# Crossbar transposes for the later tiles of a second matrix layer, and a weight load that is moved behind a scatter

## What is computed

```
h = relu(layernorm(x))
x = x + gat(relu(gat(h, W1, att1, b1)), W2, att2, b2)
h = relu(layernorm(x))
x = x + gcn(relu(gcn(h, W3, b3)), W4, b4)

gat: h = h @ W;  e = leaky_relu((h @ att_src)[src] + (h @ att_dst)[dst]);  softmax of e over the edges of one dst
     out[dst] = sum of alpha * h[src];  + b
gcn: h = h @ W;  out[dst] = sum of h[src] / sqrt(deg[src] * deg[dst]);  + b
```

## Time and profile before

| what | value |
|---|---|
| median of 3 runs | 2192.77 us (2192.68 to 2198.5) |
| profiled execution, own time | 2194.5 us |
| its span, first to last instruction | 2192.7 us |
| TensorE busy | 2143.6 us, 98% of the span |
| VectorE, ScalarE, GpSimd busy | 1461.2, 947.1, 863.9 us |
| SyncE's DMA queue, GpSimd's DMA queue | 263.74 MB and 172.60 MB, 41.5% and 25.4% of the engines' span |

### The profile page before, as it was taken

The page is one execution under the profiler, slowest core; times in us unless marked ns, Lnnn a source line. Parts: engine busy times, 40 slices in busy tenths (PEclk is TensorE's granted clock), DMA queues, the critical chain, the costliest instruction groups (busy, mean ns, idle before and its releaser), DMA issues.

```text
span 2192.7 us, 35927 instructions
## 1 busy us (share of the span) xinstructions
PE 2143.6 (98%) x13355; PEld 1359.5 (62%) x13355; DVE 1461.2 (67%) x3322; ACT 947.1 (43%) x1289; POOL 863.9 (39%) x1067
## 2 busy tenths in 40 slices
PE   8999998899999999999999999999999999999997
PEld 4666665556666666666666666666666666666664
DVE  8998753435766764343889999665666667876563
ACT  4444454344545454333554444433334333333432
POOL 3212177524333321243654454443353413245462
PEclk9999999999999999999999999999999999999999
DMA  5988999995556554434755566666766747776562
GB/s 185 234 223 200 227 214 201 184 241 158 177 191 202 187 172 134 166 122 141 241 183 200 187 203 202 225 244 220 280 238 228 238 165 252 234 246 192 176 202 85
DMA packets 243091, 438.63 MB, mean 200 GB/s; under 512 B 138867, under 2 KB 139065, under 8 KB 242790
## 3 DMA queue, kind: packets, MB, share of 16 engines
q1 hardware_dynamic: 202550, 263.74, 41.5%
q0 software_dynamic: 40368, 172.60, 25.4%
HBM read 234.94 MB, written 179.89 MB: 189 GB/s over the span
## 4 chain that ended last, share of the span: by engine, by line
PE 90%; DVE 6%; issue 2%; ACT 1%; POOL 1%; POOLq 0%; DVEq 0%; ACTq 0%
PE ps_h L993 78%; PE ps_z L969 7%; PE ps_e L1069 1%; PE ps_e L1070 1%; DVE edge_mem L1246 1%; PE ps_e L1059 1%; PE ps_e L1060 1%; DVE bn L1156 1%; DVE z_lo L1208 1%; DVE res L1235 0%; DVE res L1225 0%; ACT z L876 0%; DVE pre L1174 0%; DVE pre L1172 0%; PE ps_e L1015 0%
## 5 line engine op out<-in xcount | busy, mean ns | idle before, releaser
L993 PE MATMUL ps_h<-w_hi,z_hi 128*128 128x384 f16 x2916 | 712.9, 326 | 1.6 <-DVE w_lo L1146 1.6
L993 PE MATMUL ps_h<-w_hi,z_lo 128*128 128x384 f16 x2916 | 712.9, 326 | 0.0
L993 PE MATMUL ps_h<-w_lo,z_hi 128*128 128x384 f16 x2916 | 712.9, 326 | 0.0
L863 ACT ACTIVATE row_out<-ps_h,grow 128x768 f32<-128x768 f32 x237 | 212.9, 898 | 647.5 <-PE ps_h L993 637.9
L1208 DVE TENSOR_TENSOR z_lo<-ps_z,z_hi 128x768 f16<-128x768 f32 x243 | 231.8, 954 | 353.2 <-ACT z_hi L868 352.8
L993 PEld LDWEIGHTS ps_h<-w_lo,z_hi 128*128 128x128 f16 x2916 | 285.5, 98 | 189.1 <-issue 0.7
L993 PEld LDWEIGHTS ps_h<-w_hi,z_lo 128*128 128x128 f16 x2916 | 285.5, 98 | 189.0 <-issue 0.7
L993 PEld LDWEIGHTS ps_h<-w_hi,z_hi 128*128 128x128 f16 x2916 | 285.2, 98 | 176.0 <-issue 20.8
L993 PE MATMUL ps_h<-w_hi,x_keep 128*128 128x384 f16 x1752 | 362.6, 327 | 14.0 <-issue 14.0
L993 PEld LDWEIGHTS ps_h<-w_hi,x_keep 128*128 128x128 f16 x1752 | 169.9, 98 | 127.9 <-issue 19.5
L685 POOL DMA_INDIRECT out<-res,perm_out x79 | 103.5, 1310 | 322.6 <-DVE res L1235 301.3
(11 more groups left out here) (223 smaller groups left out, 2515.6 us busy)
## 6 DMA issues: line engine op xcount, KB each, us to landing
rows<-row_out SPq DMA_DIRECT2D x199, 384.0 KB
rows<-e_out SPq DMA_DIRECT2D x60, 384.0 KB, 4.5
row_in<-in_x SPq DMA_DIRECT2D x40, 384.0 KB, 3.8
row_in<-rows SPq DMA_DIRECT2D x40, 384.0 KB, 4.3
x_rows<-pre SPq DMA_DIRECT2D x40, 384.0 KB, 3.8
res<-x_rows SPq DMA_DIRECT2D x40, 384.0 KB, 4.2
pure_rows<-row_out SPq DMA_DIRECT2D x39, 384.0 KB
row_in<-pure_rows SPq DMA_DIRECT2D x39, 384.0 KB, 5.1
```

The costliest lines, as they stand in the source:

```text
L863: nc.scalar.activation(pair(row_out[t.slot]), psum_pair(ps_h[t.slot]), ACT.Copy, scale=scale).then_inc(row_ready, 1)
L993: last = nc.tensor.matmul(ps_h[s][:, a, 0:HALF], zp[:, c, :], wp[:, c, a * HALF:(a + 1) * HALF], start=(c == 0 and zp is zh and wp is hi), ...
```

## The change

Tiles of layer 2 from g = 124 on are crossed as well. Their preparation on VectorE and their gather on GpSimd move one window ahead. The third weight's loads move from windows 53 to 58 to windows 65, 67, ... 75, its maxima from one in each window from 59 to every second window from 68, its joining matmul from window 70 to 79, its scale to 80. Bias 1 is loaded in window 66, biases 2, 3 and 4 in windows 89, 91 and 93, each with its own semaphore that its first user waits for; the attention vectors of layer 1 move from window 69 to 74. The wait for the parameters before the degrees is taken out. The maxima of the second weight start three windows later. The small diagonal matrix of `max_w` lies in `e_out`, and the small per-tile factors have eight slots in place of four. The diff, without the repeated changes of `slot4` to `slot8`:

```diff
-        self.slot, self.slot4 = g % 2, g % 4
+        self.slot, self.slot8 = g % 2, g % 8
-        self.crossed = layer == 1 and g >= FIRST_CROSSED
+        self.crossed = layer == 1 and g >= FIRST_CROSSED or layer == 2 and g >= SECOND_CROSSED
+SECOND_CROSSED = 124
+    W3_AT = SCATTERED + 1
-    max_at = {2: TURNED + 4, 3: ORDERED + 1, 4: begin["2m"] + 14}
+    max_at = {2: TURNED + 4, 3: W3_AT + 2 + 2 * KC, 4: begin["2m"] + 14}
-        w_diag = edge_mem[:, 15 * P:16 * P]
+        w_diag = e_out[:, 512:512 + P]
...
# SyncE
                 t = tile(w, 6)
-                if t and t.crossed:
+                if t and t.crossed and t.layer == 1:
                     load_x(t)
-            def load_params():
-                for n in (1, 2, 3, 4):
-                    sp.dma_start(bias_bc[n][:, :], row_of(bias[n])).then_inc(params_loaded, 16)
+            def load_bias(n):
+                sp.dma_start(bias_bc[n][:, :], row_of(bias[n])).then_inc(bias_loaded[n], 16)
-                if w == ORDERED:
-                    load_params()
+                for n, at in ((1, ORDERED - 3), (2, ORDERED + 20), (3, ORDERED + 22), (4, ORDERED + 24)):
+                    if w == at:
+                        load_bias(n)
+                if w == ORDERED + 5:
                     load_atts(1)
-                if MASKS + 6 <= w < MASKS + 6 + KC:
-                    load_w(3, w - MASKS - 6)
+                if W3_AT <= w < W3_AT + 2 * KC and (w - W3_AT) % 2 == 0:
+                    load_w(3, (w - W3_AT) // 2)
...
# GpSimd
                 t = tile(w, 4)
-                if t:
+                if t and not t.crossed:
+                    load(t)
+                t = tile(w, 5)
+                if t and t.crossed:
                     load(t)
...
# ScalarE, make_half
+                if t.layer == 1:
+                    (as before, with the layer norm's factors)
+                else:
+                    nc.scalar.activation(z_half[t.xn % 3][:, 0:D], input_of(t)[:, :], ACT.Relu,
+                                         scale=shrink[t.slot8][:, 0:1]).then_inc(half_ready, 1)
...
# VectorE
+                    if layer == 4:
+                        dve.wait_ge(e_stored, (ET + 1) * 16)
+            def pre_free(t):
+                ago = T[t.g - 2]
+                x_read(dve, ago)
-                wait(dve, z_ready, t.g - 1)
+                pre_free(t)
                 if not t.chain:
                     wait(dve, x1_stored[t.slot], t.x1_before * 16)
+                elif t.c < KEEP:
+                    dve.wait_ge(h_ready, begin["3"])
-                dve.wait_ge(params_loaded, 16 * 4)
                 t = tile(w, 4)
                 if t and t.crossed:
-                    prepare_first(t)
+                    (prepare_first if t.layer == 1 else prepare_even)(t)
-                for layer, top_from, low_from in ((2, 19, TURNED + 6), (3, MASKS + 12, begin["2"] + 43), (4, begin["2m"] + 4, begin["3"] + 1)):
-                    if top_from <= w < top_from + KC:
-                        max_w(layer, w - top_from)
+                for layer, top_from, each, low_from in ((2, 22, 1, TURNED + 6), (3, W3_AT + 3, 2, begin["2"] + 43),
+                                                        (4, begin["2m"] + 4, 1, begin["3"] + 1)):
+                    if top_from <= w < top_from + each * KC and (w - top_from) % each == 0:
+                        max_w(layer, (w - top_from) // each)
```

More of the change, by code:

```diff
@@ L228, in build @@
     assert len(plain_at) == len(last_at) == ET
-    max_at = {2: TURNED + 4, 3: ORDERED + 1, 4: begin["2m"] + 14}
+    max_at = {2: TURNED + 4, 3: W3_AT + 2 + 2 * KC, 4: begin["2m"] + 14}
+    assert max_at[3] + 1 < EDGES[1]
     def gat_of(w):
@@ L283, in build @@
         bn = [sb(f"bn{s}", [P, 12]) for s in range(2)]
[L284 to L291, removed]
+        mv = [sb(f"mv{s}", [P, 2]) for s in range(8)]
+        veps = [sb(f"veps{s}", [P, 1]) for s in range(8)]
+        rstd = [sb(f"rstd{s}", [P, 1]) for s in range(8)]
+        nmr = [sb(f"nmr{s}", [P, 1]) for s in range(8)]
+        top = [sb(f"top{s}", [P, 1]) for s in range(8)]
+        topc = [sb(f"topc{s}", [P, 1]) for s in range(8)]
+        shrink = [sb(f"shrink{s}", [P, 1]) for s in range(8)]
+        grow = [sb(f"grow{s}", [P, 1]) for s in range(8)]
         bias_bc = {n: sb(f"bias_bc{n}", [P, D]) for n in (1, 2, 3, 4)}
@@ L378, in build @@
         consts_ready = sem("consts_ready")
-        params_loaded = sem("params_loaded")
+        bias_loaded = {n: sem(f"bias_loaded{n}") for n in (1, 2, 3, 4)}
         atts_loaded = sem("atts_loaded")
@@ L688, in norm_factors @@
             def norm_factors(t):
-                s, k = t.slot4, t.ln
+                s, k = t.slot8, t.ln
                 pool.wait_ge(mean_var, k + 1)
@@ L861, in evict @@
                     act.wait_ge(grow_ready, t.k + 1)
-                    scale = grow[t.slot4][:, 0:1]
+                    scale = grow[t.slot8][:, 0:1]
                 nc.scalar.activation(pair(row_out[t.slot]), psum_pair(ps_h[t.slot]), ACT.Copy, scale=scale).then_inc(row_ready, 1)
@@ L875, in make_z @@
                         act.wait_ge(x_loaded[t.in_slot], t.in_count * 16)
-                    nc.scalar.activation(z[t.slot][:, :], input_of(t)[:, :], ACT.Relu, bias=nmr[t.slot4][:, 0:1],
-                                         scale=rstd[t.slot4][:, 0:1]).then_inc(z_ready, 1)
+                    nc.scalar.activation(z[t.slot][:, :], input_of(t)[:, :], ACT.Relu, bias=nmr[t.slot8][:, 0:1],
+                                         scale=rstd[t.slot8][:, 0:1]).then_inc(z_ready, 1)
                 else:
@@ L880, in make_z @@
                     nc.scalar.activation(z[t.slot][:, :], input_of(t)[:, :], ACT.Relu,
-                                         scale=shrink[t.slot4][:, 0:1]).then_inc(z_ready, 1)
+                                         scale=shrink[t.slot8][:, 0:1]).then_inc(z_ready, 1)
             def make_half(t):
@@ L1158, in statistics @@
                 dve.wait_ge(stats_done, t.ln + 1)
-                V.bn_aggr(mv[t.slot4][:, :], bn[s][:, :]).then_inc(mean_var, 1)
+                V.bn_aggr(mv[t.slot8][:, :], bn[s][:, :]).then_inc(mean_var, 1)
             def prepare_first(t):
@@ L1176, in prepare_third @@
                 statistics(t, to)
-                V.tensor_scalar(grow[t.slot4][:, :], dinv_grow[:, 0, t.pos:t.pos + 1], 1.0, None, ALU.mult).then_inc(grow_ready, 1)
+                V.tensor_scalar(grow[t.slot8][:, :], dinv_grow[:, 0, t.pos:t.pos + 1], 1.0, None, ALU.mult).then_inc(grow_ready, 1)
+            first_of = {layer: min(t.g for t in T if t.layer == layer) for layer in (2, 4)}
             def prepare_even(t):
-                s, s4 = t.slot, t.slot4
+                s, s4 = t.slot, t.slot8
                 if t.loaded:
@@ L1186, in prepare_even @@
                     rows = row_out[t.of.slot]
-                wait(dve, z_ready, t.g - 1)
+                pre_free(t)
                 wait(dve, x1_stored[s], t.x1_before * 16)
                 b = bias_bc[t.layer - 1]
+                if t.g in first_of.values():
+                    dve.wait_ge(bias_loaded[t.layer - 1], 16)
                 if t.layer == 4 and t.mixed:
@@ L1233, in result @@
                         V.tensor_tensor(to[:, 0:D], row_out[t.slot][:, :], to[:, 0:D], ALU.add).then_inc(x1_used, 1)
+                if t.r == 0:
+                    dve.wait_ge(bias_loaded[4], 16)
                 dve.wait_ge(x1_used, t.r + 1)
```

6 lines of the change are left out of this document (4 added, 2 removed).

## The result

The change makes the kernel faster, but by a third of what was forecast: 2183.67 us in the median of five runs (2179.48 to 2187.59) against 2192.77 before, a ratio of 0.9949 with a 95% interval of 0.9935 to 0.9963. The forecast was 2166, its range 2156 to 2178. The profiled execution took 2187.6 us and is the slowest of the five. In all that follows, the ratios leave out two slow executions, one of 4618 us in before_with_factors and one of 2183.3 us in factors_from_100. Lines of the code have moved: the products are L1005 here, the transposes of TensorE L981, SyncE's two DMA transposes of a tile L540 (first half) and L545 (second).

What follows compares the result with a forecast made beforehand. TensorE's own work was taken to bound the kernel nearly everywhere, except a layer-1 stall from 348 to 460 us. Terms -22.3 - 4.7 - 0.8 + 0.8 = -27.0 us from 2192.8 gave 2166, range 2156 to 2178.

Steps and rivals of the forecast that it cites:

- Part 1: Layer-2 tiles from 124: the DMA, not TensorE, transposes them (crossed); 34 x 0.655 = 22.3 us gained.
- The DMA's room: Layer 2: a crossed tile asks for a DMA share of 0.77 to 1.20; cost taken as nothing.
- rivals C and D: Layer 2: last 20 tiles stay at 6.5 us, 2179 (chance 0.12); or crossed tiles take 7.56 us, 2224 (0.04).
- The burst: Fourth weight's six loads in one window at tile 135, now among crossed tiles: 0.8 us lost, bounds 0 and 3.
- signs of being wrong: Layer-2 landings past 10 us, an earlier last scatter, or TensorE's clock falling in a stretch taken at full speed.
- Part 2: Layer 1: third weight's loads moved behind the scattered rows; tile 67 starts at 430.0, 4.7 us gained.
- rival A: Layer 1: the wait in front of tile 67 takes back the whole 4.7 us gain; 2170.5 us, chance 0.16.
- rival B: Layer 1: the whole stall goes, 14.0 us of idle and 1.8 of low clock; 2155.5 us, chance 0.13.
- Part 3: Biases loaded one at a time, most in windows 89 to 93: the burst at 445.53 goes, 0.8 us gained.

Runs made afterwards that it cites:

- before_with_factors: Kernel before the change, with only two of three layer-norm factors made by VectorE in windows 44 to 63: 2190.65 us, ratio 0.9983.
- factors_from_100: factors_on_vector with layer-2 tiles crossed from 100 on: inconclusive, runs between 2146.5 and 2183.3 us, ratio 0.9857.
- no_second_crossing: The changed kernel with no tile of layer 2 crossed: 2194.09 us, ratio 1.0.
- w4_spread: The changed kernel with the fourth weight loaded one part every second window from 129 to 139, not six in window 135: 2175.58 us, ratio 0.9918.
- w3_burst: The changed kernel with all six loads of the third weight in window 69, among crossed tiles of layer 1: 2181.79 us, ratio 0.9942.
- factors_old_schedule: factors_on_vector with third weight, biases and layer-1 attention vectors loaded where the kernel before loads them: 2169.97 us, ratio 0.9894.
- factors_on_vector: w4_spread with VectorE making two of three factors for tiles whose factors GpSimd makes between its scatters (windows 44 to 63): 2164.06 us, ratio 0.9863.
- crossing_alone: The changed kernel with only the crossed tiles of layer 2 left, weights, biases and attention vectors loaded as in the kernel before: 2182.07 us, ratio 0.9956.

## Why the prediction was wrong

**Part 1's gain was right.** 34 x 0.655 was taken. The stretch that begins with the transposes of tile 123 takes 197.8 us in no_second_crossing (819.45 to 1017.21) and 178.1 in w4_spread (818.38 to 996.49), 19.65 us for its 30 crossed tiles, 0.655 each. The medians of these two are 18.5 us apart. Some 3 us of the full 22.3 are missing behind it: the profiled executions are 22.7 us apart at the first wait of the last sums (2105.57 before, 2082.90 in w4_spread) and 19.2 us at the end. The waits of those sums are 3.3 us in all before and 4.9 after; and behind the longest of them (2.69 us at 2092.06) 12 matmuls take 3.18 us in place of 1.95, at a granted clock of 0.91 in 2080 to 2100. That is most of it; why the wait is longer wasn't tried.

**The DMA's room was right in its size.** The share was put between 0.77 and 1.20 and is 1.00 at 840 to 860 us. The last 20 tiles run without a gap when no burst meets them, so rivals C and D fall.

**The burst was the first failed step.** The term, taken from a burst in layer 1, was +0.8 us with bounds 0 and 3; it is 8.1 us by the medians and 7 to 11 by the traces. A gap near tile 137 was forecast, but of this small size; two of the signs of being wrong that the prediction names came with it, landings past 10 us and a fallen clock. The row it was taken from, the burst at 445.53, is a layer-1 row: there GpSimd's queue moves nothing, and w3_burst shows that six weight parts are free in that place too. Nor did the same burst cost anything in layer 2 among turned tiles, beside the same gathers: the tiles of the kernel before keep their 6.505 us from 819.97 to 1008.61. In layer 2 every tile's rows come through GpSimd's gathers. What differs is what shares the engines, transposes and gathers together: in the changed kernel the gathers land in 3.9 us at 860 to 880 and 12.7 us behind the burst (5.0 there without it, in w4_spread), and stores and transposes are late with them. The Trainium skill (DMA: Bandwidth & Descriptors, "Issuing engines are not separate DMA queues") says that transfers of SyncE and GpSimd run on the same 16 engines and interleave. The trace agrees: behind a burst that only SyncE issued, GpSimd's gathers landed 8.8 us later. That the gathers are what turns a free burst among crossed tiles into a dear one is argued from the two places and not shown: no burst was tried in layer 2 without them, since its tiles need them, and the burst of layer 1 came behind a gap.

The tail of the burst is the other part. The weights' six issues are over at 897.3 and land in 6.1 us (median), yet transposes take 4.98 and 5.59 us to issue at 906 and 913, where none of w4_spread's takes over 2.1 us in 885 to 945. So SyncE's issuing takes longer than a tile lasts: the store at 903.34 and the two transposes behind it take 7.67 us, the store at 911.20 and its two 7.72, against 5.85. It does not wait for stores meanwhile: ScalarE's eviction ends at 908.79, and its store is issued only at 911.20, when the transpose ahead of it in the queue is out. In the stalled stretch of the kernel before it is the same: SyncE's issues fill 7.36 us of the 7.63 from 357.57 to 365.20. Whether the long issues are the cause of the late landings or only a sign of full engines was not tried. With the stall comes the clock, 0.83 in 920 to 940 us, behind the gaps of 3.4 and 4.3 us.

**Part 2 was the second.** It was taken as -4.7 and is 0: rival A, that the wait in front of tile 67 takes everything back. Two sizes were off. Tile 67's second transpose was to land 6 us after its issue. It was issued at 423.96, and tile 67 started 8.9 us later, at 432.88, past the upper bound of 8.75. And the lowered clock was allowed 1.5 us, but the 192 matmuls behind the gaps took 37.3 us (26.50 and 10.81) in place of 31.2. So the 4.8 us that tiles 55 to 66 had won were spent again, in the gap and in the clock behind it. The last scatter did stay where the prediction held it, at 414.01 us against 413.78.

**Behind part 2, the picture was incomplete, not false.** The prediction named two things that coincide, the loads and GpSimd's scatters, and then held that GpSimd alone sets 415 us. Both stall TensorE over neighbouring tiles, and whichever is left takes most of it:

| | factors on GpSimd | two factors on VectorE |
|---|---|---|
| third weight and biases early | 2193.9 (before) | 2190.7 (before_with_factors) |
| the same with crossed tiles and W4 spread | not run | 2170.0 (factors_old_schedule) |
| third weight and biases late, crossed tiles, W4 spread | 2175.6 (w4_spread) | 2164.1 (factors_on_vector) |

To move the loads alone brings nothing (no_second_crossing), the factors alone 3.2 us; the factors bring 11.5 us once the loads have moved, and the loads 5.9 us once the factors have. So most of rival B's 15.8 us of layer 1 were there to be had, but not by this change: with the factors moved too, tile 78 starts 11.0 us earlier than in the kernel before (490.31 against 501.28).

**Part 3's 0.8 us** is too small to be told in the medians: crossing_alone, which keeps the old burst of biases, is 1.6 us below the change, within the runs' spread. Its chain has no gap behind that burst (44.85 us without one from 454.94), so the 0.76 us of the earlier trace rows are not a fixed price of it.

**The sum with what was measured**: -22.3 for part 1, +8.1 to +11.2 for the burst, 0 for parts 2 and 3, some +3 at the end: -11 to -8, against 9.1 measured.

## What to carry to other kernels

A price taken from another stage need not hold where other queues are busy: before a burst is costed at nothing, look at what every queue carries in the stage where it will land, and spread it when the stage's slack is spoken for; in layer 2 here two bursts of three loads were free and one of six cost 8 us. Where two causes stall the same tiles, taking one away shows little (0 and 3.2 us here); look at the rate of each alone (6.46 us of GpSimd against 5.85 of TensorE) and try them together. An engine that is 40% busy over the span can be the bound of one stage, and moving 0.6 to 0.8 us a window off it was worth 11.5 us once the loads were out of the way.

## What was not expected of the hardware

A burst that has landed isn't over: the six loads landed in 6.1 us (median) after issues that ended at 897.3 us, but TensorE lost its time between 907 and 940. Until then SyncE's single transposes take up to 5.59 us to issue, and in 920 to 940 us the engines show a larger share than without the burst (1.19 against 0.98 in w4_spread) and move fewer bytes (156 against 212 GB/s). The two long gaps of layer 1 (3.00 and 4.39 us) cost 6 us more through the clock behind them (0.83 from 400 to 440 us), nearly as much as they lasted; the six gaps of factors_on_vector, at most 1.5 us each, have a clock of 1.00 behind them. The length of a gap alone does not tell: behind 3.37 us at 907.85 a tile took 6.01 us, behind 2.06 us in the kernel before one took 7.69.
